# Two message-passing layers on one core: the table work of later zones spread over other ticks, the places worked out across partitions, the warm-up moved ahead, the norms' products split by column

## The reference

```python
h = relu(layernorm(x))
agg0 = segment_sum(edge_attr_64 @ W_edge.T, dst) / max(degree, 1)
x = x + concat([h @ W_self.T, agg0 @ W_neigh.T]) @ W_final.T + b_final
h = relu(layernorm(x))
agg1 = segment_sum(edge_attr_128, dst)
x = x + relu(concat([h, agg1]) @ W1 + b1) @ W2 + b2
```

## Time and profile before

| | us |
|---|---|
| median of 3 runs | 556.91 (556.08 to 558.59) |
| the profiled execution | 556.97 |
| its span, first to last instruction | 555.1 |
| PE busy | 503.9 (91%) |
| DVE busy | 390.6 (70%) |
| POOL busy | 368.4 (66%) |
| ACT busy | 151.5 (27%) |
| mean granted clock of PE | 0.966 |

### The profile page before, as it was taken

How to read it: one execution, slowest core, us unless ns; L and a number is a source line. 1 busy time by engine, 2 the same in 40 slices (tenths; PEclk the granted TensorE clock), 3 DMA queues, 4 the chain that set the end, 5 groups by cost and what they waited for, 6 DMA issues and landing times.

```text
span 555.1 us, 25952 instructions
## 1 busy us (share of the span) xinstructions
PE 503.9 (91%) x10989; PEld 450.1 (81%) x10989; DVE 390.6 (70%) x1230; ACT 151.5 (27%) x353; POOL 368.4 (66%) x524
## 2 busy tenths in 40 slices
PE   5568879899989999999999999998999999999993
PEld 4457768789878898888988898888888888988782
DVE  5434698776896768967798688789669877567322
ACT  0011101332233332342234224333323332313101
POOL 2735947667577776785768777885866765845730
PEclk9767899999999999999999999999999999999996
DMA  8924999999999998999999999999999998959910
GB/s 282 388 58 148 380 354 359 374 339 322 312 347 303 341 349 303 367 301 313 341 323 355 333 331 323 369 320 304 325 320 358 329 322 277 382 221 310 378 41 13
DMA packets 113229, 169.53 MB, mean 305 GB/s; under 512 B 5486, under 2 KB 84310, under 8 KB 113111
## 3 DMA queue, kind: packets, MB, share of 16 engines
q1 hardware_dynamic: 85843, 154.42, 79.7%
q10 hardware_dynamic: 27268, 13.43, 8.3%
HBM read 161.43 MB, written 6.40 MB: 302 GB/s over the span
## 4 chain that ended last, share of the span: by engine, by line
PE 81%; issue 6%; DVE 4%; DVEq 1%; ACT 0%; POOL 0%
PE ps L631 28%; PE ps L649 15%; PE ps L694 9%; PE ps L706 5%; PE ps L633 5%; PE ps L678 5%; PE ps L669 4%; PE ps L715 4%; PE ps L708 4%; DVE agg L1043 2%; PE ps L658 1%; DVE x L1157 1%; DVE onehot L1013 1%; DVE bn L1137 0%; DVEq L1043 0%
## 5 line engine op out<-in xcount | busy, mean ns | idle before, releaser
L631 PEld LDWEIGHTS ps<-onehot,ring 128*64 128x64 f32 x3126 | 198.8, 141 | 30.8 <-issue 22.6
L631 PE MATMUL ps<-onehot,ring 128*64 128x64 f32 x3126 | 217.2, 228 | 6.5 <-issue 4.6
L633 PE MATMUL ps<-onehot,ring 128*64 128x64 f32 x3126 | 217.3, 228 | 4.7 <-issue 4.7
L522 POOL TENSOR_TENSOR hot_part<-onehot 128x384 bf16<-128x384 f32 (+2 forms) x128 | 116.7, 912 | 152.3 <-DVE onehot L1013 150.6
L633 PEld LDWEIGHTS ps<-onehot,ring 128*64 128x64 f32 x3126 | 198.8, 141 | 5.4 <-issue 5.4
L1043 DVE TENSOR_TENSOR agg<-ps,agg 128x128 f32 (+1 forms) x319 | 95.0, 298 | 120.1 <-PE ps L658 95.9
L1013 DVE TENSOR_TENSOR onehot<-iota_win,rel 128x384 f32<-128x384 f32 (+3 forms) x192 | 164.5, 857 | 0.2
L649 PE MATMUL ps<-onehot,ring 128*64 128x64 f32 x3126 | 121.9, 226 | 7.2 <-issue 7.1
L649 PEld LDWEIGHTS ps<-onehot,ring 128*64 128x64 f32 x3126 | 109.2, 141 | 7.4 <-issue 7.2
L694 PEld LDWEIGHTS ps<-w_c,agg 128*128 128x128 f32 x424 | 49.8, 191 | 7.3 <-DVE agg L1043 3.7
L694 PE MATMUL ps<-w_c,agg 128*128 128x129 f32 x424 | 52.3, 276 | 3.3 <-issue 2.3
(11 more groups left out here) (118 smaller groups left out, 568.7 us busy)
## 6 DMA issues: line engine op xcount, KB each, us to landing
ring<-in_edge_attr_dram SPq DMA_DIRECT2D x95, 768.0 KB, 5.5
ring<-in_edge_attr_dram SPq DMA_DIRECT2D x96, 384.0 KB, 7.0
ring<-in_edge_attr_dram SPq DMA_DIRECT2D x32, 832.0 KB, 6.2
ring<-in_edge_attr_dram SPq DMA_DIRECT2D x32, 416.0 KB, 7.7
x<-in_x_dram ACTq DMA_DIRECT2D x23, 256.0 KB, 6.3
out_dram<-x ACTq DMA_DIRECT2D x23, 256.0 KB
x<-in_dst_dram SPq DMA_DIRECT2D x1, 384.0 KB
x<-in_dst_dram SPq DMA_DIRECT2D x1, 208.0 KB, 3.6
```

The lines of the kernel that those rows point to most:

```text
L522: nc.gpsimd.tensor_tensor(out, a, b, ALU.add).then_inc(s_hotsum, 1)
L631: nc.tensor.matmul(bank[0:H, o:o + WIN], ring128[0:K, slot, u, 0:H], hots, start=u == 0, stop=r == R - 1, skip_group_check=True)
L633: nc.tensor.matmul(bank[H:P, o:o + WIN], ring128[0:K, slot, u, H:D], hots, start=u == 0, stop=r == R - 1, skip_group_check=True)
```

## The change

1. `relative` of zones 3, 1, 2 runs at the end of ticks 0, 3, 5; `table` at the end of ticks 1, 4, 6; `copy_table` in ticks 2, 5, 7.
2. The places are worked out on `firsts` while each chunk still has its own partition (four columns, five instructions, into `placed`), ahead of PE's turn onto one partition. Behind it is one copy. Three small instructions make the offset and the bound of each partition from `chunk_no`.
3. `ones_f` is set by DVE, so the warm-up waits for that alone, not for POOL's constants. It is 18 products of `ones_f` by `ones_f`, not 5 of `ones_f` by `ident`.
4. The one-hots of tick 1 are made ahead of the wait for the rest of `dst`, those of tick 2 behind the places.
5. In `scale_1` and `scale_2` the product is made for one column at a time, with 1/std as an operand per partition.

```diff
-    WARM_UP = 5
-    N_CONST = 10
-    COPIED_AT = (1, 2, 3)
+    WARM_UP = 18
+    N_CONST = 9
+    RELATIVE_AT, TABLE_AT, COPIED_AT = (0, 3, 5), (1, 4, 6), (2, 5, 7)
...
-        wrapped = sb("wrapped", [1, CH, 4], I16)
+        wrapped = sb("wrapped", [P, 4], I32)
+        placed = sb("placed", [P, 4])
+        is_upper = sb("is_upper", [P, 1])
+        put_at = sb("put_at", [P, 1])
...
-                    nc.tensor.matmul(ps[:, 2, 0:P], ones_f[:], ident[:], start=True, stop=True)
+                    nc.tensor.matmul(ps[:, 2, 0:P], ones_f[:], ones_f[:], start=True, stop=True)
...
-                    last = nc.tensor.matmul(ps_base[:, b * CH:(b + 1) * CH], firsts[:, b:b + 1], ident[:], start=True, stop=True)
+                    last = nc.tensor.matmul(ps_base[:, b * CH:(b + 1) * CH], placed[:, b:b + 1], ident[:], start=True, stop=True)
...
+            pe.wait_ge(s_ones, 1)
+            warm_up()
             pe.wait_ge(s_const, N_CONST)
-            warm_up()
             table(0)
...
-                if t < 3:
-                    table(ZONES[t + 1])
+                if t in TABLE_AT:
+                    table(ZONES[TABLE_AT.index(t) + 1])
...
-                nc.vector.scalar_tensor_tensor(nmr1[:, u, 0:nt], mv1[:, u, 0:nt, 0], -1.0, rstd1[:, u, 0:nt], ALU.mult,
-                                               ALU.mult).then_inc(s_nmr1, 1)
+                for j in range(nt):
+                    last = nc.vector.tensor_scalar(nmr1[:, u, j:j + 1], mv1[:, u, j, 0:1], rstd1[:, u, j:j + 1], -1.0, ALU.mult, ALU.mult)
+                last.then_inc(s_nmr1, 1)
...
             nc.vector.memset(dst_i[96:128, LAST_E:12 * P], 0).then_inc(s_dst_clear, 1)
+            nc.vector.memset(ones_f[:], 1.0).then_inc(s_ones, 1)
             nc.vector.memset(agg[:, :, 0:START_CLEAR], 0.0).then_inc(s_zero, 1)
+            dve.wait_ge(s_const, N_CONST)
+            link(nc.vector.tensor_scalar(is_upper[:], chunk_no[:], float(SPLIT), None, ALU.is_ge))
+            nc.vector.tensor_scalar(put_at[:], is_upper[:], float(UPPER_AT - FIRST_W), float(FIRST_W), ALU.mult, ALU.add)
+            link(nc.vector.tensor_scalar(is_upper[:], is_upper[:], 16384.0, None, ALU.mult))
...
             one_hots(0)
+            one_hots(1)
             dve.wait_ge(s_dst, 80)
...
-            nc.vector.memset(nviol[:], 0.0).then_inc(s_firsts, 1)
-            for t in range(1, AHEAD):
+            link(nc.vector.tensor_scalar(placed[:], firsts[:], 0.0, 16383.0, ALU.max, ALU.min))
+            link(nc.vector.tensor_scalar(wrapped[:], placed[:], float(FIRST_W), float(FIRST_W), ALU.max, ALU.subtract))
+            nc.vector.tensor_scalar(placed[:], placed[:], is_upper[:, 0:1], None, ALU.add)
+            link(nc.vector.tensor_scalar(wrapped[:], wrapped[:], 4 * GW - 1, None, ALU.bitwise_and))
+            nc.vector.scalar_tensor_tensor(placed[:], wrapped[:], put_at[:, 0:1], placed[:], ALU.add, ALU.min).then_inc(s_firsts, 1)
+            for t in range(2, AHEAD):
                 one_hots(t)
             dve.wait_ge(s_psbase, 1)
-            nc.vector.tensor_scalar(base[0:1, :, :], ps_base.rearrange("p (b c) -> p c b", b=4), 0.0, 16383.0, ALU.max,
-                                    ALU.min).then_inc(s_base, 1)
+            nc.vector.tensor_copy(base[0:1, :, :], ps_base.rearrange("p (b c) -> p c b", b=4)).then_inc(s_base, 1)
             dve.wait_ge(s_base, 1)
-            nc.vector.tensor_scalar(wrapped[0:1, :, :], base[0:1, :, :], float(FIRST_W), float(FIRST_W), ALU.max, ALU.subtract).then_inc(s_base, 1)
...
-            dve.wait_ge(s_base, 5)
...
-                    if t < 3:
-                        relative(ZONES[t + 1])
+                    if t in RELATIVE_AT:
+                        relative(ZONES[RELATIVE_AT.index(t) + 1])
```

More of the change, by code:

```diff
@@ L336, in build_gnn @@
         s_const, s_dve, s_passed = sem("s_const"), sem("s_dve"), sem("s_passed")
-        s_dst_clear, s_dst0, s_dst, s_firsts, s_rel, s_tab, s_untab, s_base = (
-            sem(n) for n in ("s_dst_clear", "s_dst0", "s_dst", "s_firsts", "s_rel", "s_tab", "s_untab", "s_base"))
+        s_dst_clear, s_ones, s_dst0, s_dst, s_firsts, s_rel, s_tab, s_untab, s_base = (
+            sem(n) for n in ("s_dst_clear", "s_ones", "s_dst0", "s_dst", "s_firsts", "s_rel", "s_tab", "s_untab", "s_base"))
         s_psbase, s_w, s_wps, s_wsb = (sem(n) for n in ("s_psbase", "s_w", "s_wps", "s_wsb"))
@@ L455, in _ @@
                                  allow_small_or_imprecise_dtypes=True))
-            const(nc.gpsimd.memset(ones_f[:], 1.0))
             const(nc.gpsimd.memset(ones_h[:], 1.0))
@@ L1148, in scale_2 @@
                 dve.wait_ge(s_rstd2, q + 1)
-                nc.vector.scalar_tensor_tensor(nmr2[:, u, 0:nt], mv2[:, u, 0:nt, 0], -1.0, rstd2[:, u, 0:nt], ALU.mult,
-                                               ALU.mult).then_inc(s_nmr2, 1)
+                for j in range(nt):
+                    last = nc.vector.tensor_scalar(nmr2[:, u, j:j + 1], mv2[:, u, j, 0:1], rstd2[:, u, j:j + 1], -1.0, ALU.mult, ALU.mult)
+                last.then_inc(s_nmr2, 1)
             def result(q):
@@ L1170, in _ @@
             nc.vector.tensor_copy(firsts[64:96, 3:4], dst_i[64:96, 0:1])
+            nc.vector.memset(nviol[:], 0.0)
             link(nc.vector.tensor_copy(firsts[96:128, 0:4], dst_i[96:128, 0:12 * P:3 * P]))
-            nc.vector.memset(nviol[:], 0.0).then_inc(s_firsts, 1)
-            for t in range(1, AHEAD):
+            link(nc.vector.tensor_scalar(placed[:], firsts[:], 0.0, 16383.0, ALU.max, ALU.min))
[4 more added lines that the diff above has]
+            for t in range(2, AHEAD):
                 one_hots(t)
             dve.wait_ge(s_psbase, 1)
-            nc.vector.tensor_scalar(base[0:1, :, :], ps_base.rearrange("p (b c) -> p c b", b=4), 0.0, 16383.0, ALU.max,
-                                    ALU.min).then_inc(s_base, 1)
+            nc.vector.tensor_copy(base[0:1, :, :], ps_base.rearrange("p (b c) -> p c b", b=4)).then_inc(s_base, 1)
             dve.wait_ge(s_base, 1)
-            nc.vector.tensor_scalar(wrapped[0:1, :, :], base[0:1, :, :], float(FIRST_W), float(FIRST_W), ALU.max, ALU.subtract).then_inc(s_base, 1)
[L1181 to L1186, removed]
-            dve.wait_ge(s_base, 5)
             places = {0: load_bases(ORDER[0])}
```

## The result

The kernel after takes 552.76 us (median of 20 runs, 549.43 to 556.73), the kernel before, run beside it, 558.17 (20 runs, 552.59 to 565.64): a ratio of 0.9926, interval 0.9900 to 0.9952. That is 0.74% faster, 4.1 us of the 556.91 us given at the start, where 19.9 us were forecast. The time lies outside the range of 530 to 545 us. The profiled execution took 555.99 us with a span of 554.1.

A forecast was written before the change was run, and what follows sets the result against it. PE was taken as the bound, with time lost to its stops in the opening. The smaller of 20.4 (DMA) and 21.3 us (DVE), less about 0.5 and 0.1, gave 19.9: 556.97 - 19.9 = 537.1 us, range 530 to 545.

The forecast's parts named there:

- The waits that go: Opening: PE's four waits at L583, 16.1 us, fall under 8; no PE idle over 3 us between 11 and 50.
- Warm-up and table(0): Kernel start: eighteen products start near 2.3 us and end near 9.5; table(0) comes over 1 us later.
- the same pace afterwards: From the point where 105 us was: same work and pace, the lead kept, not enlarged.
- The DVE and PE line: Opening, tick by tick through sums, tables and adds: adds(8) start 21.3 us earlier.
- Adds(8) near 46: End of the opening: adds of tick 8 start near 46 us, against 67.32 before.
- the loosest: The PE line in the opening: with warm clock and no stops, tick 4 ends 25 us earlier.
- The DMA line: Loads from 25 to 55 us: 3.63 MB takes 9.6 us at 379 GB/s, putting an unpaused stream 20.4 us ahead.
- The sum: Whole kernel: smaller of 20.4 and 21.3, less about 0.5 and 0.1, gives 19.9 us gained, 537.1 us.
- Rival (b): Opening: stream runs dry, PE waits for `relative`, clock falls, slots late; gain 8 to 12, 545 to 549 us; chance 0.15.
- (a): Opening to 105 us: PE line carries more, DMA at 399 GB/s, lead 28 us, time 529; chance 0.12.
- (c): Norm products, 105 to 540 us: 1.03 us each, four a norm, make DVE the bound; 591 us; chance 0.02.
- Rival (d): Opening: stops only change place, late table(0) and lost early one-hots cancel the gain; 556 us; chance 0.02.

The follow-up runs named there:

- tiny ones: Thirteen one-column products added behind the five warm-up products of the kernel before with only the tick tuples changed: 553.09 us, ratio 0.9952.
- unshifted: The kernel before with only the three tuples of ticks changed and no tiny products added: 541.91 us, ratio 0.9748.

## Why the prediction was wrong, point by point

- *The waits that go.* Right: four waits of 16.1 us became 4.1 ("under 8 us"), no idle time of PE over 3 us is left between 11 and 50 us (the longest 2.28), adds(0) came at 19.03 (17.6 to 19.7 said).
- *Warm-up and table(0).* First product at 1.91 (2.3 said), 36 records end at 8.0, table(0) 0.5 us later where "over 1 us" was said. The place computations fitted: `base` copied at 17.43. Small terms, rightly small. But here lies the failed step that matters: the thirteen products were costed only by the time that they take at the start. They also move all the work behind them by 52 instructions against the blocks in which PE's instructions come, and that cost some 10 us (five instead of 18: 9.6 by the ratios, 10.7 by the medians) and 11.2 (tiny ones); all of the change but the ticks cost 12. No term or rival held it, and the forecast "the same pace afterwards" fell by it.
- *The DVE and PE line.* "Adds(8) near 46": 55.82, and 53.84 without loads. The step that failed is the sequence from sums(2) on, laid out at 2.3 us a chunk and then called "the loosest" on PE's side. PE ran sums(2) at the low level (24.3 to 28.9, 4.6 us) and had 14.8 us at that level between 25 and 55 us, worth 7.4 us. The clock there is 0.75, not above 0.9. PE, not DVE, was the late line: DVE is busy 16.81 of these 30 us.
- *The DMA line.* It was the smaller of the two terms and so set the sum, wrongly: it isn't a bound. In the kernel before the features of ticks 3 to 7 had landed 14 to 24.5 us before their first matmul, those of ticks 8 to 11 still 4.1 to 6.8 us, and past the first chunk PE waits for no load in either kernel. A DMA share of 1.06 from 55 to 80 us is a ring being refilled, not a stream that holds the engine up. The kernel before used that stock to run from tick 3 to tick 8 in 16.0 us, where the kernel after needed 23.2. Its only stop over 1 us there is one of the grid, not one for a load:
```profile
59.36 0.41 PE L649 MATMUL ps<-onehot,ring 128*64 128x64 f32 x2 [1.86 <-issue]
```
The gain of the ticks is therefore not the length of the pauses in the loads, 20.4, but 13.5 us measured: a lead of 17.9 us at tick 3, less what the moved work and the low clock take behind it.
- *The sum.* 19.9 us said. By the ratios of the runs, with parts taken off one at a time: 14.0 us for the ticks, -0.3 (not to be told from 0) for places, early start, order and norms, -9.6 for the thirteen products, 4.1 for the whole. With five warm-up products the time, 542.05 us, would have lain in the range, but by luck: the DMA line, from which the sum was taken, would have been as wrong.
- *Rival (b)*, 545 to 549 us, was nearest, in its mechanism too (short stops, low clock, slots late), though its clock sank by far less than it feared and its stops were mostly not for `relative`. Rivals (a) and (c) fell: 207 ns for the products that (c) put at 1.03 us. Rival (d) fell too, though at 552.8 us the time is nearer to its 556 than to the forecast; what cancelled the gain was neither the late table(0) nor the one-hots. (The wait that (d) gives as 6.99 us is that of the weight load; the matmul's, in the prediction's own rows, is 6.70.)

## What to carry to other kernels

A wait that is filled by moving work out of a chain is worth its length less what the moved work costs where it lands: look whether the stretch behind the stop now runs on a stock (landings far ahead of their use), for there the old kernel catches up. In this kernel, with PE over 90% busy beside loads of 306 to 314 GB/s in the mean, the same work differed by 2% with the number of instructions ahead of it. Before an edit that adds or removes PE instructions is judged, compare the "issue" waits and the granted clock of the profiles, and try it with a few idle products more or less. A change of several parts is best measured part by part: here one part held the whole gain and another took about 70% of it back.

## What the runs showed of the hardware

- PE's stream shifted by 52, 128, 180 and 256 instructions: 553.1, 548.3, 546.6 and 543.0 us, against 541.9 unshifted.
- The stops, up to 3.1 us each, come only with the loads beside them. Without later loads the kernel after takes 21.3 us less by the medians, the kernel before 17.7, with the same number of instruction packets. They stand on a grid of about 253 matmuls and weight loads in PE's stream, which is the block of the page quoted above but for PE's other instructions, and each ends 1.1 to 1.6 us behind the landing of a packet. "Mostly hidden" holds by count, since 11 to 22 of some 87 crossings show a stop of 0.3 us or more, but these stops make up most of the 14 to 28 us of "issue" waits in each kernel with all its loads.
- What makes a fetch late at one crossing and not at another is open, as is why a position costs what it costs; the packets' own durations, 1.0 us, don't change. No trace here has a record of the fetch unit itself. That the stops are waits for instructions rests on the landings, the grid, the return at 256 and the kernels without later loads.
- Time that stops cost comes with time at the lower clock level: with 13 tiny products, 7.2 us more of stops came with 5.2 us more lost to the clock. It isn't a fixed price: with 32, the stops are as long (21.2 us) and the clock is at 0.980.
